# A transformer block with two attentions: six casts moved from DVE to ScalarE, an addition to GpSimd, gate rows double-buffered, and 85 pipeline steps placed anew

## The reference

```python
c_proj = jax.nn.silu(c) @ W_mod + b_mod
shift_a, scale_a, gate_a, shift_m, scale_m, gate_m = jnp.split(c_proj, 6, axis=-1)
x_norm = modulate(_ln(x), shift_a, scale_a)
q, k, v = jnp.split(x_norm @ W_qkv + b_qkv, 3, axis=-1)        # 16 heads
attn_w = jax.nn.softmax(jnp.einsum('bhqd,bhkd->bhqk', q, k) * scale, axis=-1)
attn_out = jnp.einsum('bhqk,bhkd->bhqd', attn_w, v)             # heads put side by side
x = x + gate_a[:, None] * (attn_out @ W_proj + b_proj)
q_c = _ln(x) @ W_qc + b_qc
k_c, v_c = jnp.split(_ln(context) @ W_kvc + b_kvc, 2, axis=-1)
x = x + cross_attention(q_c, k_c, v_c) @ W_cproj + b_cproj
h = jax.nn.gelu(modulate(_ln(x), shift_m, scale_m) @ W_mlp1 + b_mlp1)
x = x + gate_m[:, None] * (h @ W_mlp2 + b_mlp2)
```

## Time and profile before

| | before |
|---|---|
| median of 3 runs | 1712.57 us (1707.13 to 1715.95) |
| the profiled execution's own time | 1710.94 us |
| its span in the trace | 1709.1 us |
| busy: PE, DVE, ACT, POOL | 1414.3, 1289.2, 1045.4, 690.7 us |
| mean granted TensorE clock | 0.952 |

### The profile page before, as it was taken

The page is one execution under the profiler, slowest core; times in us unless marked ns, Lnnn a source line. Parts: engine busy times, 40 slices in busy tenths (PEclk is TensorE's granted clock), DMA queues, the critical chain, the costliest instruction groups (busy, mean ns, idle before and its releaser), DMA issues.

```text
span 1709.1 us, 40543 instructions
## 1 busy us (share of the span) xinstructions
PE 1414.3 (83%) x15090; PEld 924.8 (54%) x15090; DVE 1289.2 (75%) x2701; ACT 1045.4 (61%) x2151; POOL 690.7 (40%) x973
## 2 busy tenths in 40 slices
...
DMA packets 166117, 138.07 MB, mean 81 GB/s; under 512 B 45921, under 2 KB 156674, under 8 KB 165922
## 3 DMA queue, kind: packets, MB, share of 16 engines
...
## 4 chain that ended last, share of the span: by engine, by line
PE 26%; DVE 24%; SPq 22%; DMA 10%; issue 9%; POOL 5%; ACT 3%; POOLq 0%; ACTq 0%; DVEq 0%
SPq L436 12%; SPq L469 8%; DVE mx_self L988 8%; PE dense_ps L351 6%; PE dense_ps L353 5%; PE dense_ps L352 5%; DVE mx_cross L988 4%; DMA o_rb_cross<-r_dram_cross 4%; PE max_ps L643 3%; PE o_ps L678 3%; DVE ot_self L1002 2%; DMA o_d_self<-o_sb_self 2%; DMA o_rb_self<-r_dram_self 2%; POOL o_n_cross L1108 2%; DVE xt L950 2%
## 5 line engine op out<-in xcount | busy, mean ns | idle before, releaser
L799 ACT ACTIVATE probs<-exp_ps 128x512 f32<-128x512 f32 x1024 | 558.4, 602 | 377.1 <-PE exp_ps L660 374.3
L988 DVE TENSOR_REDUCE mx_cross<-max_ps 128x2 f32<-128x512 f32 x512 | 329.1, 685 | 120.9 <-PE max_ps L643 120.4
L988 DVE TENSOR_REDUCE mx_self<-max_ps 128x2 f32<-128x512 f32 x512 | 326.8, 679 | 30.8 <-PE max_ps L643 30.7
L643 PE MATMUL max_ps<-k_stack_self,q_stack_self 48*128 48x256 f16 x1024 | 105.2, 285 | 97.5 <-DVE mx_self L988 60.4
L1136 POOL TENSOR_TENSOR g_split<-G,g_split 128x512 f16<-128x512 f32 x128 | 148.2, 1168 | 64.4 <-DVE g_split L1026 64.4
L351 PE MATMUL dense_ps<-xt,mlp_hi 128*128 128x256 f16 x512 | 141.3, 276 | 6.4 <-DVE xt L950 6.4
L351 PE MATMUL dense_ps<-mlp_hi,g_split 128*128 128x256 f16 x512 | 141.6, 277 | 3.5 <-POOL g_split L1136 3.5
L678 PE MATMUL o_ps<-probs,V_cross 128*32 128x256 f32 x2048 | 141.7, 396 | 0.0
L678 PE MATMUL o_ps<-probs,V_self 128*32 128x256 f32 x2048 | 141.4, 395 | 0.0
L352 PE MATMUL dense_ps<-mlp_lo,g_split 128*128 128x256 f16 x512 | 140.9, 275 | 0.0
L353 PE MATMUL dense_ps<-mlp_hi,g_split 128*128 128x256 f16 x512 | 140.9, 275 | 0.0
...
## 6 DMA issues: line engine op xcount, KB each, us to landing
q_stack_self<-split_q SPq DMA_DIRECT2D x192, 64.0 KB, 2.6
k_stack_self<-split_k SPq DMA_DIRECT2D x192, 64.0 KB, 2.6
q_stack_cross<-split_qc SPq DMA_DIRECT2D x192, 64.0 KB, 2.6
k_stack_cross<-split_kc SPq DMA_DIRECT2D x192, 64.0 KB, 2.7
...
o_rb_self<-r_dram_self SPq DMA_DIRECT2D x256, 32.0 KB, 1.8
```

Of the source, the lines that this page charges most:

```text
L643: mm = pe.matmul(max_ps[:, ab, qt * T:(qt + 1) * T], q_stack[kind][rows, b.u, p, qt * P:(qt + 1) * P], k_stack[kind][rows, b.u, p], start= ...
L799: nc.scalar.activation(probs[:, (t + ab) % 8], exp_ps[:, ab], ACT.Exp).then_inc(exp_taken[kind], 1)
L988: nc.vector.tensor_reduce(mx[kind][:, :, ab, t // 2], max_ps[:, ab].rearrange("p (q k) -> p q k", q=2), AX_X, ALU.max).then_inc(max_taken[ ...
```

## The change

DVE loses six casts per batch. Four, from `G` to `g_split`, become `gelu_hi` on ACT and stand inside the GELU block, each behind the next pair of GELUs; two, `o_hi_self` and `o_hi_cross`, become steps of ACT, and DVE keeps their remainders as steps `o_lo_self` and `o_lo_cross`. The addition of XR into X2 goes from DVE to POOL as the step `x2_add`. `rows_a` and `rows_b` get two buffers, and SP's waits ahead of their loads look one batch further back. 85 steps have new places (lag, half, slot), most banks new users, and the loop has one more iteration (`LAST` 37).

```diff
 PLAN = {
-    "q": (-1, 1, 6), "q_hi": (-1, 1, 7), "k": (-1, 1, 9), "k_hi": (-1, 1, 8), "stack_k": (-1, 1, 12), "v": (-1, 1, 9),
-    "o_gather_cross": (3, 1, 5), "r_back_cross": (3, 1, 15), "o_hi_cross": (4, 0, 2), "cproj": (4, 0, 5),
-    "mlp1_0": (4, 0, 14), ... "gelu": (4, 0, 15), "mlp2_3": (4, 1, 14), "store": (4, 1, 15), ...
+    "q": (-1, 1, 1), "q_hi": (-1, 1, 3), "k": (-1, 1, 6), "k_hi": (-1, 1, 6), "stack_k": (-1, 1, 10), "v": (0, 0, 7),
+    "o_gather_cross": (3, 1, 10), "r_back_cross": (4, 0, 1), "o_hi_cross": (4, 0, 4), "cproj": (4, 0, 6),
+    "mlp1_0": (4, 1, 0), ... "gelu": (4, 1, 0), "mlp2_3": (5, 0, 2), "store": (5, 1, 3), ...
 }
-FIRST, LAST = -1, 36
+FIRST, LAST = -1, 37
...
-        rows_a = sb("rows_a", [P, 2, D])
-        rows_b = sb("rows_b", [P, 2, D])
+        rows_a = sb("rows_a", [P, 2, 2, D])
+        rows_b = sb("rows_b", [P, 2, 2, D])
...
                     if (b := due("rows_a")):
-                        sp_wait(taken["proj"], b.n)
+                        sp_wait(taken["proj"], b.n - 1)
                     if (b := due("rows_b")):
-                        sp_wait(taken["mlp2"], b.n)
+                        sp_wait(taken["mlp2"], b.n - 1)
...
+            def gelu_hi(b, i):
+
+                act.wait_ge(taken[f"mlp1_{i}"], b.n + 1)
+                nc.scalar.activation(g_split[:, 0, 2 * i:2 * i + 2], G[:, 2 * i:2 * i + 2], ACT.Copy).then_inc(g_hi, 1)
...
+                    for kind in KINDS:
+                        if (b := due(f"o_hi_{kind}")):
+                            act.wait_ge(o_mult[kind], b.n + 1)
+                            wait_count(act, ready["proj" if kind == "self" else "cproj"], b.n)
+                            nc.scalar.activation(ot[kind][:, 0], o_n[kind][:], ACT.Copy).then_inc(ot_hi[kind], 1)
...
                     if (b := due("gelu")):
                         wait_count(act, g_lo, b.n * 4)
+                        wait_count(act, ready["mlp2"], b.n)
...
                             last.then_inc(taken[f"mlp1_{i}"], 1)
+                            if i:
+                                gelu_hi(b, i - 1)
+                        gelu_hi(b, 3)
...
-                            nc.vector.tensor_copy(ot[kind][:, 0], o_n[kind][:]).then_inc(ot_hi[kind], 1)
+                        if (b := due(f"o_lo_{kind}")):
...
-                            nc.vector.tensor_copy(g_split[:, 0, 2 * i:2 * i + 2], G[:, 2 * i:2 * i + 2]).then_inc(g_hi, 1)
...
-                        dve.wait_ge(taken["proj"], b.n + 1)
-                        dve.wait_ge(xr_done, b.n + 1)
-                        nc.vector.tensor_tensor(X2[:, b.u], X2[:, b.u], XR[:], ALU.add).then_inc(x2_done, 1)
...
+                    if (b := due("x2_add")):
+                        pool.wait_ge(taken["proj"], b.n + 1)
+                        pool.wait_ge(xr_done, b.n + 1)
+                        nc.gpsimd.tensor_tensor(X2[:, b.u], X2[:, b.u], XR[:], ALU.add).then_inc(x2_done, 1)
```

More of the change, by code:

```diff
@@ L35 @@
 PLAN = {
[L36 to L45, removed]
@@ L46 @@
-    "stack_kc": (2, 0, 14), "vc": (2, 0, 15), "vc_hi": (2, 1, 0), "split_cross": (3, 0, 0), "m_cross": (3, 0, 0),
-    "m_copy_cross": (3, 0, 2), "o_gather_cross": (3, 1, 5), "o_recip_cross": (3, 1, 11), "r_out_cross": (3, 1, 6),
-    "r_back_cross": (3, 1, 15), "o_norm_cross": (3, 1, 9), "o_hi_cross": (4, 0, 2), "cproj": (4, 0, 5),
[6 rows of a table removed]
+    "load_x": (-1, 0, 0), "ln1": (-1, 0, 4), "norm1": (-1, 0, 6), "t1": (-1, 0, 8), "t1_hi": (-1, 0, 9),
+    "t1_lo": (-1, 0, 10), "q": (-1, 1, 1), "q_hi": (-1, 1, 3), "q_lo": (-1, 1, 4), "stack_q": (-1, 1, 8),
@@ new lines @@
+    "k": (-1, 1, 6), "k_hi": (-1, 1, 6), "k_lo": (-1, 1, 8), "stack_k": (-1, 1, 10), "v": (0, 0, 7),
+    "v_hi": (0, 0, 8), "split_self": (0, 0, 15), "m_self": (0, 1, 0), "m_copy_self": (0, 1, 0),
+    "o_gather_self": (1, 0, 13), "o_recip_self": (1, 0, 13), "r_out_self": (1, 0, 14), "r_back_self": (1, 0, 14),
+    "o_norm_self": (1, 0, 14), "o_hi_self": (1, 1, 4), "o_lo_self": (1, 1, 7), "rows_a": (0, 1, 7),
+    "xr": (0, 1, 12), "proj": (1, 1, 9), "x2": (1, 1, 11), "x2_add": (1, 1, 11), "ln2": (1, 1, 13),
@@ new lines @@
+    "norm2": (1, 1, 14), "t2": (2, 0, 1), "t2_hi": (2, 0, 1), "t2_lo": (2, 0, 2), "qc": (2, 0, 5),
+    "qc_hi": (2, 0, 5), "qc_lo": (2, 0, 6), "stack_qc": (2, 0, 8), "xc": (3, 1, 10), "load_c": (0, 0, 14),
+    "lnc": (0, 0, 15), "normc": (0, 1, 7), "tc": (1, 0, 14), "tc_hi": (1, 0, 14), "tc_lo": (1, 0, 15),
+    "kc": (1, 1, 3), "kc_hi": (1, 1, 7), "kc_lo": (1, 1, 9), "stack_kc": (2, 0, 5), "vc": (2, 0, 10),
+    "vc_hi": (2, 0, 11), "split_cross": (3, 0, 0), "m_cross": (3, 0, 0), "m_copy_cross": (3, 0, 2),
@@ L55 @@
+    "o_gather_cross": (3, 1, 10), "o_recip_cross": (3, 1, 13), "r_out_cross": (3, 1, 13),
+    "r_back_cross": (4, 0, 1), "o_norm_cross": (4, 0, 1), "o_hi_cross": (4, 0, 4), "o_lo_cross": (4, 0, 4),
[5 rows of a table added]
 }
 BANK = {
-    "m_self": 1, "m_cross": 2, "qc": 1, "cproj": 0, "tc": 1, "kc": 2, "t3": 2, "mlp1_0": 1, "mlp1_1": 2,
-    "mlp1_2": 0, "mlp1_3": 1, "vc": 0, "t1": 1, "proj": 0, "mlp2": 2, "q": 1, "k": 0, "v": 1, "t2": 0,
+    "m_self": 2, "m_cross": 0, "qc": 2, "cproj": 0, "tc": 0, "kc": 1, "t3": 1, "mlp1_0": 1, "mlp1_1": 0,
@@ L60 @@
+    "mlp1_2": 2, "mlp1_3": 1, "vc": 1, "t1": 0, "proj": 0, "mlp2": 1, "q": 0, "k": 2, "v": 1, "t2": 2,
 }
@@ L419, in load_rows @@
                 row = src[b.n:b.n + 1].rearrange("a r d -> a (r d)")
-                nc.sync.dma_start(dst[:].rearrange("p r d -> p (r d)"), row.to_broadcast([P, 2 * D])
+                nc.sync.dma_start(dst[:, b.u].rearrange("p r d -> p (r d)"), row.to_broadcast([P, 2 * D])
                                   ).then_inc(s[b.u], 16)
@@ L998, in at @@
                             nc.vector.reciprocal(o_r[kind][:], o_d[kind][:]).then_inc(o_recip[kind], 1)
-                        if (b := due(f"o_hi_{kind}")):
-                            dve.wait_ge(o_mult[kind], b.n + 1)
-                            wait_count(dve, ready["proj" if kind == "self" else "cproj"], b.n)
-                            nc.vector.tensor_copy(ot[kind][:, 0], o_n[kind][:]).then_inc(ot_hi[kind], 1)
+                        if (b := due(f"o_lo_{kind}")):
                             dve.wait_ge(ot_hi[kind], b.n + 1)
```

14 lines of the change are left out of this document (5 added, 9 removed), and 11 rows, old and new, of the table PLAN.

## The result

| | before | after |
|---|---|---|
| median | 1709.85 us of 4 (1705.99 to 1715.95) | **1631.21 us** of 4 (1629.31 to 1634.88) |
| ratio | 1 | **0.9548**, 95% interval 0.9523 to 0.9572 |
| profiled execution, its span | 1710.94, 1709.1 us | 1633.06, 1631.3 us |
| busy: PE, DVE, ACT, POOL | | 1406.4, 1145.2, 1130.6, 718.4 us |

What follows compares the result with a forecast made beforehand. No engine is full; PE's waits on other engines and SP's queue bound the kernel. Iterations save 55.6 us, the fill 6, the drain 0: span 1709.1 to 1647.5, so 1650 us, range 1612 to 1695.

Steps and rivals of the forecast that it cites:

- the walk: One iteration of the new order priced slot by slot, each group at the later of input and engine: 45.2 us clean.
- the even part: The 27 iterations between the fifth and last `mt_self` copy: 47.66 us each before, forecast 45.6, saving 55.6 us.
- the fill: The stretch before the even part: norm1 and t1 stand in the first half, saving 6 us (0 to 15).
- the drain: The stretch behind the even part: two extra hops against a freer DVE, 0 (±5) us.
- The stacked keys: PE's 1.16 us wait ahead of the first self maxima goes, the keys landing about 3 us before they are needed.
- The cross chain: `o_d_cross` through SP to cproj, behind twelve DMAs: 13 us, input ready about 0.3 us before PE gets there.
- the slower rival: GELU, stacks and cross chain close a slower loop through SP, decisive from 2.1 us late: 1742 us, chance 0.10.
- The wait for `probs`: New PE wait at exponents of (1,4), after ACT's GELU block with four casts (7.9 us): 1.8 us, bounds 0.9 to 3.5.
- DVE's relief: DVE loses 4.3 us of about 40 per batch; not the gain, because DVE waits for PE elsewhere.
- The gate rows: Double buffers let SP's waits look one batch further back; worth nothing in itself.
- The rule weighed: A DVE cast beside POOL's work lasts to the other's end (1226 against 427 ns); such meetings counted as nothing.
- The port-lock rival: New POOL addition and two DVE differences block each other on shared ports: 1.3 us an iteration, 1685 us, chance 0.10.

Runs made afterwards that it cites:

- e6: The changed kernel with stack_k one slot later, so SP gathers the cross attention's sums and values ahead of k's six DMAs: 1666.67 us.
- e10: The changed kernel with one buffer for each kind of gate rows, their loads later, and X's load and ln1 later too: 1690.87 us.
- e5: The changed kernel with the third and fourth g_split casts back on DVE: 1603.67 us, timed again at 1607.29 us.
- e4: The changed kernel with all four g_split casts back on DVE: 1604.07 us.
- e12: The changed kernel with all four g_split casts on DVE and a small unused exponential behind the last GELU, so the table load comes early: 1598.99 us.
- e1: The changed kernel's new places, with all six casts and the addition into X2 back on DVE: 1616.80 us.
- e3: The changed kernel with only the addition into X2 back on DVE: 1632.44 us.
- e9: The changed kernel with the third and fourth g_split casts and the addition into X2 back on DVE: 1610.02 us.
- e8: The changed kernel with one buffer for each kind of gate rows, the loads moved behind their last use: 1752.11 us.
- e2: The changed kernel's engines and row buffers with the places, banks and LAST of the kernel before: 1760.59 us.
- e11: The changed kernel with the third and fourth g_split casts and the cast o_hi_cross on DVE: 1602.50 us.

## Why the prediction was right, and where it wasn't

1650 us was forecast, 1612 to 1695, and 1631.21 is measured. The places and the queue work in the main as the walk has them. The forecast span is 16.2 us too long: the even part gave 7.0 us more than forecast and the fill 20.6 more, and the drain took 11.4 back. So the total is nearer than its terms by luck, and a third term's size too came out by some luck (point 4).

*The even part* was forecast at 45.6 us and is 45.35: 62.6 us instead of 55.6. The sum had 42.1 us of work and of the 0.1 at each group, and 3.1 us of waits, or 3.5 with the disturbed iterations; the profile has 42.07 us of PE's busy time and 3.28 idle. Of the kernel before, though, the prediction gave numbers only for the waits for the keys (0.92 us in the mean) and `ot_cross` (0.73); of the 5.35 us idle `mx_self` made 1.36 and `xn` 0.65. By its points:

1. The stacked keys: right in place and size (1.16 us in the clean iteration, 0.92 in the mean). e6 shows the same mechanism from the other side.
2. The cross chain, 13 us from `o_d_cross` to cproj: measured 13.0. The input was to be 0.3 us early and is 0.50 late in the clean iteration. That a loop closes through SP was the slower rival's point, and e10 bears it out, though PE's added wait there is for a DMA behind the chain's and not for `ot_cross`; its decisive delay of 2.1 us didn't come: q's and k's issues took 3.81 and 4.23 us where it needed 4.7 each, and the GELU block grew from 6.02 us to 7.69 (898.27 to 905.96), where 7.9 was forecast.
3. The self side: right. The 20.3 us that PE waited before for `ot_self` ahead of proj are 0.0 in the changed kernel's groups.
4. The wait for `probs`: forecast 1.8, measured 1.42, and 37.7 / 27 = 1.40 in the mean of the even part. What the walk had wrong is its cause: I laid all of it to the four casts. e5 and e4 show that they make about 0.65 of it, and e12 that a table load behind a wait makes the rest. That the size came near all the same is luck in part.

*DVE's relief* was priced at nothing, since DVE waits for PE elsewhere. Right, and e1 goes further: with all of it back on DVE the kernel is faster, by the casts in the GELU block. Also *the addition*, priced at nothing, is worth nothing (e3, e9).

*The gate rows* were said to be worth nothing in themselves. That sentence fell. At the new places they let SP load rows at a place where the load doesn't stand in the cross chain; without them the kernel takes 1691 to 1752 us (e10, e8), so at these places most of the change's gain goes with them. e10 and e8 are two placings only; a better one with single buffers was not searched for.

*The fill* is the term that was mis-sized: forecast 6 us, bounds 0 to 15, measured 26.6. *The drain* was forecast 0 ± 5 and lost 11.4. Part of both is one thing: the stretch before the fifth `mt_self` copy holds one MLP block less than before, the stretch behind the last one more. GELU's line, eight activations and a load to a block, has 45 instructions in the drain of the changed kernel, five blocks, and only one, a load, in the fill; before, there were four blocks in the drain (36) and one in the fill (9). That part nets to nothing. Net of both, fill and drain gave 15.2 us where I said 6. The places make it: e2, with the old ones, has 244.8 and 183.2 us. The fill's four iterations between the first and the fifth `mt_self` copy took 144.0 us for 172.6 before, and PE's waits in them for the stacked keys, 5.7 us on the DMA and 8.3 us ahead of maxima with no releaser named, are 1.1 us in its whole execution now. So the wait that was costed for the even part was missing from the fill's sum: 12.9 of the 28.6 us. The clock may have a part in the rest. Its granted share in these four iterations was 0.79 before and 0.84 after:

```profile
72.74:245.32 172.58, 121.43 (x1136) 68.13 (x1136) 105.38 (x227) 83.66 (x173) 45.07 (x72) 0.79 0.23 68
74.76:218.75 143.99, 112.43 (x1098) 61.84 (x1097) 100.61 (x222) 81.53 (x171) 46.15 (x74) 0.84 0.27 83
```

PE's busy time there fell by 9.0 us; some of that is the 38 matmuls fewer. The remaining 7 us or so, and what holds the drain, I didn't take apart.

*The rule weighed.* That the first cast shares its time with a POOL subtraction stands in the trace of before (28 of its 32 executions lie beside one, of `g_split`), but not in the earlier trace rows, which the prediction names for it. Such meetings happen in the new order too: `ot_self`'s difference, 692 ns in the kernel before, has a mean of 993 in this one:

```profile
L1015 DVE TENSOR_TENSOR ot_self<-o_n_self,ot_self 128x512 f16<-128x512 f32 x32 | 31.8, 993 | 1.4 <-ACT ot_self L817 1.4
```

The new addition is not the one that it mostly meets, though: with it on DVE (e3) the mean is still 912, beside POOL's work on `XC`. And other meetings went: the second `mh_cross` instruction of DVE has a mean of 365 ns, and had 1210 before. The port-lock rival's 1.3 us an iteration didn't come. The Trainium skill, "SBUF — State Buffer", section "SBUF: two separate sides", says that when a DVE instruction with two SBUF inputs and a GpSimd instruction that reads SBUF meet, the one that started first keeps the shared ports for its whole length and the other waits; by that rule the trace agrees in 993 against 692. What the runs add is that such meetings move about with the order, and that here they cost nothing that a measurement tells (45.41 us an iteration in e3, 45.35 in the change).

*The best versions* among those run are e4, e5, e11 and e12, 1599 to 1607 us, which these measurements don't tell apart: 6% faster than before, and 1.5 to 2% faster than the change. Their lesson is in which engine a cast goes to: not the one whose block PE is waiting out.
